# Graph convolution after a ConvNeXt block: products of 64 stationary columns for the contraction, the projection and the distances, and y stored by image before window

## The reference

```python
h = conv_general_dilated(x, conv_w, padding=3, feature_group_count=24) + conv_b
h = layernorm(h over channels) * ln_g + ln_b
h = gelu(einsum('bhwc,cf->bhwf', h, w1) + b1)
h = einsum('bhwf,fc->bhwc', h, w2) + b2
x = h * layer_scale + x

y = affine(conv1x1(x, fc1_w, fc1_b), fc1_s, fc1_t)
nodes = window_partition(y, 8)                  # (windows, 64 nodes, 24 channels)
xn = nodes / norm(nodes)
dist = sq - 2.0 * einsum('bnc,bmc->bnm', xn, xn) + sq.T
idx = top_k(-dist, 9)
x_j = nodes[idx]
feat = concatenate([x_i, x_j - x_i])
h = gelu((einsum('bnkc,oc->bnko', feat, ew) + eb) * es + et)
h = max(h over k)
y = affine(conv1x1(window_reverse(h), fc2_w, fc2_b), fc2_s, fc2_t)
return y + x
```

## Time and profile before

| | us |
|---|---|
| median of 3 runs | 2242.76 |
| lowest and highest | 2237.08, 2244.7 |
| the profiled execution | 2235.85 |
| its span, first to last instruction | 2233.8 |
| PE busy | 1990.3 (89%) |
| DVE busy | 1525.1 (68%) |
| ACT busy | 1115.5 (50%) |
| POOL busy | 642.8 (29%) |

### The profile page before, as it was taken

One profiled execution on the slowest core, in us unless ns is written; L12 is line 12 of the kernel. 1 busy time (PEld: TensorE's weight loads), 2 busy tenths in 40 slices (PEclk: granted clock), 3 DMA queues, 4 the chain that ended last, 5 costly groups with the idle time before them and its releaser, 6 DMA issues.

```text
span 2233.8 us, 45679 instructions
## 1 busy us (share of the span) xinstructions
PE 1990.3 (89%) x13970; PEld 1041.8 (47%) x13970; DVE 1525.1 (68%) x5840; ACT 1115.5 (50%) x2630; POOL 642.8 (29%) x407
## 2 busy tenths in 40 slices
PE   6998999999789888889888988888888898989986
PEld 2444555555344444444444444444444444544442
DVE  4222222222188888888788888888888797888887
ACT  0102444344356655555555555555555565655563
POOL 3002444444122222222222222322222232222232
PEclk9997999999799999999999999999899999999899
DMA  7872333333210111111111111111111111111110
GB/s 143 148 145 62 82 78 77 76 77 78 55 20 14 34 30 33 32 33 32 33 32 33 32 33 33 33 32 33 32 33 32 30 29 28 30 25 27 29 35 16
DMA packets 225814, 105.49 MB, mean 47 GB/s; under 512 B 195904, under 2 KB 222784, under 8 KB 225472
## 3 DMA queue, kind: packets, MB, share of 16 engines
q1 hardware_dynamic: 225600, 102.63, 21.8%
HBM read 54.40 MB, written 28.90 MB: 37 GB/s over the span
## 4 chain that ended last, share of the span: by engine, by line
PE 54%; issue 19%; ACT 13%; DVE 8%; POOL 5%; SPq 1%; DMA 1%; POOLq 0%; ACTq 0%; DVEq 0%
PE bank L1059 9%; PE bank L867 7%; PE bank L924 6%; PE bank L918 6%; PE bank L992 5%; ACT xam L496 4%; PE bank L1014 4%; DVE red L783 4%; PE bank L1030 3%; PE bank L892 3%; PE bank L962 2%; POOL hq L369 2%; ACT pb L512 2%; PE bank L901 2%; PE bank L955 2%
## 5 line engine op out<-in xcount | busy, mean ns | idle before, releaser
L783 DVE TENSOR_REDUCE red<-bank 128x64 f32<-128x512 f32 x1176 | 751.8, 680 | 163.8 <-PE bank L1059 145.8
L512 ACT CAST pb<-bank 64x192 bf16<-64x192 f32 x1176 | 367.3, 312 | 375.4 <-PE bank L1030 360.4
L1059 PE MATMUL bank<-onehot,pb 128*32 128x512 bf16 x7056 | 533.2, 408 | 18.5 <-issue 16.7
L369 POOL TENSOR_TENSOR hq<-red,arena 128x384 f32<-128x384 f32 x196 | 200.9, 1025 | 554.6 <-DVE red L783 539.3
L350 POOL TENSOR_TENSOR rs<-ve,mhalf 112x16 f32<-112x16 f32 x56 | 162.4, 2899 | 377.8 <-DVE ve L689 377.8
L770 DVE TENSOR_SCALAR onehot<-slot 128x256 bf16<-128x256 bf16 x1568 | 252.9, 231 | 0.0
L1059 PEld LDWEIGHTS bank<-onehot,pb 128*32 128x32 bf16 x7056 | 137.9, 98 | 207.9 <-issue 104.1
L1001 PE MATMUL bank<-arena,wqs 128*128 128x448 f32 x336 | 171.8, 595 | 42.3 <-DMA arena<-yb 38.6
L1014 PE MATMUL bank<-xb,xam 128*128 128x64 f32 x1568 | 205.8, 277 | 0.0
L1014 PEld LDWEIGHTS bank<-xb,xam 128*128 128x128 f32 x1568 | 201.8, 201 | 2.8 <-issue 2.5
L361 POOL TENSOR_TENSOR rn<-nv,mhalf 128x28 f32<-128x28 f32 x28 | 134.5, 4805 | 229.3 <-DVE nv L742 229.3
(11 more groups left out here) (92 smaller groups left out, 2719.7 us busy)
## 6 DMA issues: line engine op xcount, KB each, us to landing
arena<-yb SPq DMA_DIRECT2D x336, 56.0 KB, 2.1
arena<-in_x SPq DMA_DIRECT2D x24, 392.0 KB
ht<-conv_d SPq DMA_DIRECT2D x112, 84.0 KB
xt<-in_x SPq DMA_DIRECT2D x112, 84.0 KB
x_d<-x1o SPq DMA_DIRECT2D x112, 84.0 KB
ht<-x_d SPq DMA_DIRECT2D x112, 84.0 KB
xt<-x_d SPq DMA_DIRECT2D x56, 168.0 KB, 3.2
out<-x1o SPq DMA_DIRECT2D x112, 84.0 KB, 2.0
```

Source lines behind the costliest of these rows:

```text
L369: nc.gpsimd.tensor_tensor(hq[:, :, :, :], red[:, k, :, :, :], qs[:, b, :, wx, :].unsqueeze(1).broadcast_to([128, 2, T, NN]), ALU.add).then ...
L512: last = nc.scalar.copy(pb[64 * u:64 * u + 64, k, part, :, :, u, :], src[64 * u:64 * u + 64, :, :, :])
L783: nc.vector.tensor_reduce(red[:, k, h, t, :], src, axis=mybir.AxisListType.X, op=op).then_inc(s["red_done"], 1)
L1059: last = mm(bank[32 * q:32 * q + 32, (k + t) % 2, :], pb[:, k, part, g, c, :, :].rearrange("p u o -> p (u o)"), onehot[:, k, g, :, :].rear ...
```

## The change

Nothing of what is computed changes. There are four edits.

1. `yb` is stored as (u, window, node) instead of (window, u, node). `make_y` writes 448 floats in a row; each copy of `load_y2` reads and writes one run of 448 floats for each of 32 partitions, before 7 runs of 64. POOL's `scale_y` reads y, and ACT's `square_y` writes its squares, in the old order by a strided pattern.
2. `contract` becomes four products of 64 stationary columns, by halves 0, 1, 0, 1 with the blocks t = 0, 1, 1, 2. `project` becomes two (one for each u), `dist` eight instead of four. Each half writes its own 64 partitions.
3. `fc1` of u = 0 moves from the middle of wx6 to the end of wx5, that of u = 1 from the end of wx6 to the middle. `make_y` of u = 0 comes behind the first `split` of wx6, u = 1 behind the third; `square_y` moves from wx0 to the end of the wx6 before.
4. On DVE `norms` moves behind the second reduction and `top8`. In wx3 the last `halfsq` goes ahead of `project`.

The diff:

```diff
         outs = x1o[:, :, :].rearrange("p (b u) l -> p b u l", b=2)
-        yb = sb("yb", [128, 2, WX, 2, NN])
+        yb = sb("yb", [128, 2, 2, WX, NN])
         xa = sb("xa", [128, 2, WX, 2, NN])
...
                         g, u = (t, 3)[blk // 2], blk % 2
-                        sp.dma_start(y2[32 * blk:32 * blk + 32, b, t, :, :], yb[32 * g:32 * g + 32, b, :, u, :]
+                        sp.dma_start(y2[32 * blk:32 * blk + 32, b, t, :, :], yb[32 * g:32 * g + 32, b, u, :, :]
                                      ).then_inc(y2_in[b], 16)
...
                 pool.wait_ge(s["rnt_done"], 2 * i + (k + 1))
-                nc.gpsimd.tensor_tensor(xa[:, b, lo:hi, :, :].rearrange("p w u i -> p (w u i)"),
-                                        rnt[:, lo:hi, :, :].rearrange("p w u i -> p (w u i)"),
-                                        yb[:, b, lo:hi, :, :].rearrange("p w u i -> p (w u i)"), ALU.mult
+                nc.gpsimd.tensor_tensor(xa[:, b, lo:hi, :, :], rnt[:, lo:hi, :, :],
+                                        yb[:, b, :, lo:hi, :].rearrange("p u w i -> p w u i"), ALU.mult
                                         ).then_inc(s["xa_done"], 1)
...
-            def make_y(i, b, banks=(6, 7)):
-                for u in range(2):
+            def make_y(i, b, us=(0, 1), banks=(6, 7)):
+                for u in us:
                     act.wait_ge(s["fc1_mm"], 2 * i + (u + 1))
-                    nc.scalar.activation(yb[:, b, :, u, :], bank[:, banks[u], 0:L].rearrange("p (w i) -> p w i", w=WX),
-                                         ACT.Identity, bias=c1[:, 0:1],
+                    nc.scalar.activation(yb[:, b, u, :, :].rearrange("p w i -> p (w i)"), bank[:, banks[u], 0:L], ACT.Identity, bias=c1[:, 0:1],
                                          scale=P("s1")).then_inc(s["y_done"], 1)
...
                 act.wait_ge(s["y_done"], 2 * (i + 1))
-                nc.scalar.activation(sq2[:, :], yb[:, b, :, :, :].rearrange("p w u i -> p (w u i)"), ACT.Square
+                nc.scalar.activation(sq2[:, :].rearrange("p (w u i) -> p u w i", w=WX, u=2), yb[:, b, :, :, :], ACT.Square
                                      ).then_inc(s["ysq_done"], 1)
...
                     split(n + 1, (r + 1) % 2, 0, s["p_mm"], s["hi_done"])
-                if pre and wx == 0:
-                    square_y(i + 1, (b + 1) % 2)
+                if early and wx == 6:
+                    make_y(i + 2, b, us=(0,))
                 if ahead1:
...
                     split(n + 1, (r + 1) % 2, 2, s["res2_mm"], s["lo_done"])
+                if early and wx == 6:
+                    make_y(i + 2, b, us=(1,))
                 if pre and wx == 2:
...
                 if early and wx == 6:
-                    make_y(i + 2, b)
+                    square_y(i + 2, b)
...
                     best(n - 2, r % 2, i - (wx < 2), (wx - 2) % WX, ((r - 2) % (2 * WX)) // WX, first)
-                if pre and wx == 0:
-                    norms(i + 1)
                 if pre and wx == 1:
...
                         dve.wait_ge(s["t8_done"], G * (n + 4))
+                if pre and wx == 0:
+                    norms(i + 1)
                 if gather:
...
                 at_least(pe, x1_dn, m - 1)
-                for t in range(3):
-                    pe.wait_ge(gelu_d, 3 * m + (t + 1))
-                    last = mm(bank[:, 6 + r % 2, 0:L], w2s[:, t, :], gl[:, t, :], start=t == 0, stop=t == 2)
+                pe.wait_ge(gelu_d, 3 * m + 2)
+                for half, t in ((0, 0), (1, 1), (0, 1), (1, 2)):
+                    if t == 2:
+                        pe.wait_ge(gelu_d, 3 * m + 3)
+                    last = mm(bank[64 * half:64 * half + 64, 6 + r % 2, 0:L], w2s[:, t, 64 * half:64 * half + 64],
+                              gl[:, t, :], start=t == half, stop=t == half + 1)
                 last.then_inc(mm2_d, 1)
...
                         t = 2 * gp + u
-                        last = mm(bank[:, 2, t * NN:(t + 1) * NN],
-                                  xam[:, b, wx, u, 2 * gp:2 * gp + 2, :].rearrange("p g i -> p (g i)"),
-                                  xb[:, b, wx, u, :], start=False, stop=True, skip_group_check=True)
+                        for h in range(2):
+                            last = mm(bank[64 * h:64 * h + 64, 2, t * NN:(t + 1) * NN], xam[:, b, wx, u, 2 * gp + h, :],
+                                      xb[:, b, wx, u, :], start=False, stop=True, skip_group_check=True)
                 last.then_inc(s["dist_mm"], 1)
...
                 at_least(pe, s["lo_done"], n)
-                both = yb[:, b, wx, :, :].rearrange("p u i -> p (u i)")
-                mm(bank[:, 3, 0:G * O], both, wp[:, :], start=True, stop=False, skip_group_check=True
-                   ).then_inc(s["p_mm"], 1)
+                for u in range(2):
+                    last = mm(bank[64 * u:64 * u + 64, 3, 0:G * O], yb[:, b, u, wx, :], wp[:, :], start=True, stop=False,
+                              skip_group_check=True)
+                last.then_inc(s["p_mm"], 1)
...
                 if early and wx == 6:
-                    fc1(i + 2, b, j + 1, 0)
+                    fc1(i + 2, b, j + 1, 1)
                 for e in qa:
...
                     fc2(i - 1, bn, 1)
-                if early and wx == 6:
-                    fc1(i + 2, b, j + 1, 1)
+                if early and wx == 5:
+                    fc1(i + 2, b, j + 1, 0)
                 for e in qb:
                     node_terms(i + 1, bn, j + b, e)
+                if pre and wx == 3:
+                    halfsq(i + 1, bn, 1, 1)
                 if ahead2:
                     project(n + 2, i + (wx + 2) // WX, r2 // WX, r2 % WX)
-                if pre and wx == 3:
-                    halfsq(i + 1, bn, 1, 1)
                 if ahead1:
```

## The result

| | before | changed |
|---|---|---|
| median, us | 2241.01 (4 runs) | 2189.16 (4 runs) |
| lowest and highest | 2237.08, 2244.7 | 2185.37, 2190.33 |
| ratio to before | | 0.9766, 95% interval 0.9744 to 0.9788 |
| span of the profiled execution | 2233.8 | 2187.2 |

52 us faster; the forecast was 2185 us. The total came out almost exactly. Its largest term did not: the wait for y2, worth 48 us in the forecast, is still there and has grown.

The account below looks back on a forecast made before the run. PE alone was taken to bound the MLP stage, PE and DVE in turn the graph stage. Terms -48 - 5 + 7 - 20 - 7 + 15 = -58 us from the median 2242.76 gave 2185 us, own range 2155 to 2215.

Parts of the forecast that it names:

- What bounds the kernel: PE alone in the MLP stage; PE and DVE waiting in turn in the graph stage; DMA wait every second iteration, 38.6 us.
- Part 1: New layout of y: y2 copies issued in 304 ns instead of 608, the wait in wx1 goes, -48 us.
- "nothing": Bound of the y2 layout's gain in wx1 if landing, not issuing, is late; the other bound was -57 us.
- The third rival: The DMA wait is replaced: the y layout gives 5 us instead of 48, total 2228 us; chance 0.12.
- its first branch: y2 lands as late as before, since SBUF to SBUF copies do not suffer from short runs; shared chance 0.12.
- Part 2: Earlier norm on PE, later `norms` on DVE: waits of 0.4 us saved in 13 slots, -5 us.
- Part 3: fc1 one place earlier: wx5 gets 0.75 us longer, wx6 gives back 0.27, 14 times, +7 us.
- Part 4: Halves of 64 columns: contract -20 us, dist -7 us, project +15 us.
- neighbours-only overlap: Contract in the MLP step: records wait in their own half, only neighbours overlap, -0.18 us a step.
- the low bound: dist in the graph stage with full overlap of the halves: -0.26 us each; -0.05 was taken.
- the forecast's case in which loads take turns: dist in the graph stage: 16 loads of 53 ns one after another are the same 0.85 us, no gain.
- The sum: Whole kernel: -48 - 5 + 7 - 20 - 7 + 15 = -58 us, giving 2185 us.

Follow-up runs that it names:

- b_y2_by_t: One semaphore for each third of the y2 copies instead of one for all twelve, against the kernel before: 2195.53 us, ratio 0.9802.

## Why the prediction was right in total and wrong in its largest term

- *What bounds the kernel* held: PE alone in the MLP stage, PE and DVE in turn in the graph stage, with the wait for y2 in every second iteration.
- *Part 1, -48 us: wrong.* The step that failed is "the new copies have 32 runs each, so I take 304 ns". It took the price of issuing from loads out of DRAM and gave it to copies from SBUF to SBUF, on the idea that runs set the price. They don't: an issue took 608 ns with 224 runs, 590 with 32, 714 with 24 (median of 336 each). I had named "nothing" as the bound and given this rival 0.12; with no row of a copy between two places in SBUF but the one to be changed, that was too little. What the wait cost was sized well: 44 us came off when it alone was removed (b_y2_by_t), and what PE lost behind it was its clock: the gather at 1264.61 in the kernel before took 1.47 us, where 0.83 is its time at full clock. The third rival is thus what happened to this part, by its first branch, though not its 2228 us. The Trainium skill ("DMA: Bandwidth & Descriptors", on why small descriptors are slow) says that short runs don't hurt such copies; the trace agrees, with 2.1 us from issue to landing for 7 runs a partition and 2.0 for one.
- *Part 2, -5 us:* nothing measurable in this kernel (norms early: ratio 0.9783 against 0.9766, within the intervals). Not costed was that a saved wait ahead of a standing one is waited away in it, nor what the clock does to the slot. The forecast had its 5 us in the middle of the body and nothing behind the turn; when the wait for y2 was gone, in a version without the new layout, the move brought 17 us, nearly all of it behind the turn. POOL's later root did fit, by the margin the forecast had: DVE waited 0.20 us for it in the slot looked at.
- *Part 3, +7 us:* the price in wx5 is as computed (8.15 to 7.40 when undone, 0.75), but wx6 in the middle gave nothing back, where the forecast had 0.27. Its floor for DVE, 6.53 us, was read in the last slots of the kernel; in wx6 DVE is busy 6.62 of 6.80 us (1318.56 to 1325.36), and the slot takes 6.80 with one product of `fc1` in it as with two. The total (undoing it brought 4 to 6 us) is inside what can be told here.
- *Part 4.* The mechanism (halves of fp32 products overlap) was right, two sizes were off to the same side. Contraction: -0.36 a step forecast, -0.52 measured, 29 to 32 us instead of 20; the forecast took the middle between full and neighbours-only overlap, and the overlap was full. Distances: -0.05 forecast, -0.23 measured, 24 to 26 us instead of 7: the low bound was right. Its sixteen records start in pairs too, and a pair follows the other by 0.05 to 0.06 us, the time that 64 columns stream. Sixteen loads one after the other at half of 0.105 us would be 0.84, and 0.62 stands there. That agrees with the Trainium skill ("TensorEngine Tiling (Array Packing)", Key Properties), by which different tiles load in parallel; the forecast's case in which loads take turns does not fit. Project: +0.15 forecast, +0.15 measured, but the slots show it in wx5 alone (7.48 to 7.63; wx4 stayed at 6.92), so it was some 4 us in 26 slots and not 15 in 98.
- *The sum.* With part 1 at zero the rest of the forecast makes -10 us. The contraction and the distances brought 26 to 31 us more than that, and the slot behind the loop's turn some 1.5 us in each of the turns, which nobody forecast and of which half was waited away again. The parts don't add up, though: halves alone give 59 us, the layout alone 14, and together with the rest they give 52. That gains ahead of the wait for y2 are partly waited away is one reason. The agreement at 2185 and 2189 is luck: errors that cancel.

## What to carry to other kernels

A wait for the last of a batch of transfers is worth splitting by consumer before anything is done to make the transfers cheaper: here that was 44 to 79 us for three lines. As long as such a wait stands, savings ahead of it can measure as nothing, so take the wait away first and test the others (norms late: 0 with it; 17 us without it, in another version) again afterwards. And when a slot's length varies from turn to turn, look at the granted clock in it before its instructions. Here products in 32-bit floats with zeros in a third or half of their stationary side gained from halves of 64 columns; the projection, which has none, paid for them.

## What the runs showed of the hardware that I had not expected

- SP's time to issue a copy from SBUF to SBUF: 608 ns for 32 partitions of 7 runs, 590 for 32 of one run, 714 for 24 of one run; a load from DRAM of 48 runs is issued in 304.
- Two fp32 products on the two halves of the array overlap wholly, records of 448 and of 64 columns alike: their records start in pairs 0.007 us apart, four products of 0.75 us take 1.65 (and 0.2 more in the product behind), sixteen records of `dist` 0.62.
- The slot after the turn of PE's loop varied between versions from 7.80 to 12.12 us by the median. Ahead of it or in it PE stands still in one wait or two of 1 to 3.3 us without a semaphore; in or behind such a wait the granted clock fell to 0.50 in most turns. With one wait and `norms` late the slot takes 6.67 us where the clock held and 9 to 10.6 where it was down for most of it.
